# Four row additions as accumulating DMAs, and two moves around W2 and the neighbour matrix, in a four-layer graph kernel

## The reference, cut to what matters

```
x1 = x0 + LN2(h1 + ff) * g2 + be2          # layer 0: attention over the edges gives h1, then
     h1 = LN1(h + att @ Wo + bo) * g1 + be1
     ff = relu(h1 @ W1 + b1) @ W2 + b2      # W1 512 x 1024, W2 1024 x 512
x2 = x1 + h @ wc + mean_over_edges(h @ wn) + bias     # layer 1, h = relu(LN3(x1))
x3 = x2 + two best of four experts, each two rounds of mean-over-edges   # layer 2
x4 = x3 + relu(degree-weighted sum of (h @ W + b))    # layer 3
```

## Time and profile before

| | us |
|---|---|
| median of 3 runs (lowest to highest) | 477.36 (476.39 to 477.62) |
| the profiled execution, its own time | 475.42 |
| its span, first to last instruction | 473.3 |
| PE busy | 450.0 (95% of the span) |
| DVE, ACT, POOL busy | 315.1, 190.5, 165.7 |

### The profile page before, as it was taken

One profiled execution on the slowest core, in us unless ns is written; L12 is line 12 of the kernel. 1 busy time (PEld: TensorE's weight loads), 2 busy tenths in 40 slices (PEclk: granted clock), 3 DMA queues, 4 the chain that ended last, 5 costly groups with the idle time before them and its releaser, 6 DMA issues.

```text
span 473.3 us, 5934 instructions
## 1 busy us (share of the span) xinstructions
PE 450.0 (95%) x2096; PEld 327.8 (69%) x2096; DVE 315.1 (67%) x570; ACT 190.5 (40%) x265; POOL 165.7 (35%) x110
## 2 busy tenths in 40 slices
PE   7999999979899998799999999999999999999996
PEld 3456544434359886678778788888888888888765
DVE  5999868999997986958865935342262237133864
ACT  5898734555133421252632353044303342227230
POOL 4000221212233996266242444144444444344100
PEclk9999999999999999799999999999999999999999
DMA  8760000000031244004011222222220332020002
GB/s 276 190 258 1 1 2 0 24 0 0 1 111 46 89 152 156 6 16 182 3 26 64 90 89 90 89 89 112 89 90 13 117 149 77 24 89 1 0 1 89
DMA packets 22474, 34.34 MB, mean 73 GB/s; under 512 B 5680, under 2 KB 5936, under 8 KB 22448
## 3 DMA queue, kind: packets, MB, share of 16 engines
q1 hardware_dynamic: 22160, 33.85, 20.3%
q10 hardware_dynamic: 288, 0.13, 0.1%
HBM read 32.93 MB, written 1.05 MB: 72 GB/s over the span
## 4 chain that ended last, share of the span: by engine, by line
PE 70%; DVE 18%; issue 6%; ACT 2%; POOL 1%; DVEq 1%; DMA 1%; POOLq 0%
PE ps L1236 15%; PE ps L1238 15%; PE ps L1237 15%; PE ps L1298 4%; PE ps L1309 4%; PE ps L1265 3%; PE ps L1264 3%; DVE rsum L947 2%; PE ps L1386 2%; DVE stats L754 2%; PE ps L1291 2%; DVE e_sb L384 2%; DVE one_src L828 1%; PE ps L1249 1%; PE ps L1565 1%
## 5 line engine op out<-in xcount | busy, mean ns | idle before, releaser
L463 POOL TENSOR_TENSOR w_lo<-w_stage,w_hi 128x1024 fp32r<-128x1024 f32 x22 | 53.6, 2434 | 129.7 <-ACT w_hi L554 118.9
L554 ACT ACTIVATE w_hi<-w_stage 128x2048 fp32r<-128x2048 f32 x23 | 43.9, 1909 | 61.8 <-PE ps L1238 61.8
L464 POOL TENSOR_TENSOR w_lo<-w_stage,w_hi 128x1024 fp32r<-128x1024 f32 x22 | 57.3, 2604 | 0.0
L1236 PE MATMUL ps<-w_hi,hid_hi 128*128 128x512 f32 x128 | 49.9, 390 | 0.5 <-DVE hid_lo L1147 0.5
L1237 PE MATMUL ps<-w_lo,hid_hi 128*128 128x512 f32 x128 | 49.8, 389 | 0.0
L1238 PE MATMUL ps<-w_hi,hid_lo 128*128 128x512 f32 x128 | 49.8, 389 | 0.0
L1236 PE MATMUL ps<-T_hi,w_hi 128*128 128x512 f32 (+1 forms) x112 | 41.0, 366 | 0.4 <-POOL w_lo L464 0.4
L1237 PE MATMUL ps<-T_lo,w_hi 128*128 128x512 f32 (+1 forms) x112 | 40.2, 359 | 0.0
L1238 PE MATMUL ps<-T_hi,w_lo 128*128 128x512 f32 (+1 forms) x112 | 40.2, 359 | 0.0
L1145 DVE TENSOR_SCALAR tmp<-ps,bl 128x512 f32<-128x512 f32 x16 | 12.0, 749 | 39.9 <-ACT hid_hi L705 39.9
L828 DVE TENSOR_SCALAR one_src<-iota_n,edge_m,edge_w 128x256 f16 x128 | 34.1, 334 | 0.4 <-POOL edge_w L500 0.4
(11 more groups left out here) (216 smaller groups left out, 998.2 us busy)
## 6 DMA issues: line engine op xcount, KB each, us to landing
w_stage<-in_L_gnn_Wr SPq DMA_DIRECT2D x8, 1024.0 KB, 5.0
w_stage<-in_L_gnn_Wl SPq DMA_DIRECT2D x8, 1024.0 KB, 5.0
w_stage<-in_L_gnn_W SPq DMA_DIRECT2D x5, 1024.0 KB, 6.6
x_sb<-in_x SPq DMA_DIRECT2D x4, 256.0 KB, 3.7
w_q<-in_L_gnn_Wq SPq DMA_DIRECT2D x1, 1024.0 KB, 7.6
w_k<-in_L_gnn_Wk SPq DMA_DIRECT2D x1, 1024.0 KB, 10.0
w_v<-in_L_gnn_Wv SPq DMA_DIRECT2D x1, 1024.0 KB, 5.9
w_o<-in_L_gnn_Wo SPq DMA_DIRECT2D x1, 1024.0 KB, 10.3
```

The costliest lines, as they stand in the source:

```text
L463: gp.tensor_tensor(w_lo[s][:, 0:2], stage[s][:, 0:2], f32(w_hi[s][:, 0:2]), ALU.subtract)
L464: gp.tensor_tensor(w_lo[s][:, 2:4], stage[s][:, 2:4], f32(w_hi[s][:, 2:4]), ALU.subtract)\
L554: nc.scalar.activation(w_hi[u % 2][:], stage[u % 2][:], ACT.Copy).then_inc(hi_made, 1)
L1236: nc.tensor.matmul(goal, a_hi, b_hi, start=start, stop=False, **kw)
```

## The change

Four things are changed.

1. The additions of `bo`, `b2` and `be2` leave POOL's arithmetic. Each becomes one DMA of 1 MB that POOL issues: it reads the 2 KB row from HBM once for every partition and tile, and adds to what is in SBUF. `be2` is issued once LN0 has read `x_sb`, and `bo` once layer 0's transposes have read `h_sb`, both behind the split of W1A; `b2` is issued where its first tile was added. Each has one completion, which DVE waits for in every tile.
2. `bias` becomes four such DMAs of 256 KB, one for each tile, each with its own semaphore. Tile `t - 1` is issued behind the power of LN3's tile `t`, and tile 3 behind that, ahead of `split_lo(WC)`. Each waits until LN3's `normalise` has read its tile. The four rows are no longer loaded by SP, and the row of `g2` no longer waits for `bo`.
3. The degree product moves from between W2A and W2B to behind the reach product, and from PSUM bank 4 to bank 6. Its copy out moves from DVE to ACT, which also moves the copy of the reach result: both now stand behind LN3's `normalise` of tile 0. PE waits for the degree copy ahead of the transposes of tile 2.
4. WN's high and low parts get buffers of their own, where the attention's third exponential buffer was. They wait only for the attention's last use of it (`pv_done`) and no longer for W2A's products. The first expert's matrix then waits for W2A's buffer.

```diff
+    w_hi.append(place("wn_hi", [P, 4, D], F32R, rVZ + 2 * MAT))
+    w_lo.append(place("wn_lo", [P, 4, D], F32R, rVZ + 3 * MAT))
...
+        def w_free(u, first):
+            if u < 2:
+                return first
+            if u == WN:
+                return pv_done, 2 * STEPS
+            return w_spent[u - 4] if u == WN + 2 else w_spent[u - 2]
+        def home(u):
+            return 2 if u == WN else u % 2
...
+            def add_bias1(t):
+                gp.wait_ge(ln_out, ln_out_no(LN3, t))
+                gp.dma_start(x_sb[:, t, :], d["L1_gnn_bias"].unsqueeze(0).to_broadcast([P, D]), accum_op=ALU.add)\
+                  .then_inc(bias1_added[t], 16)
...
+            def add_row(name, target, done):
+                gp.dma_start(target[:], d[name].unsqueeze(0).unsqueeze(0).to_broadcast([P, NT, D]),
+                             accum_op=ALU.add).then_inc(done, 16)
...
             split_lo_tile(W1A, DT - 1)
+            gp.wait_ge(ln_out, ln_out_no(LN0, NT - 1))
+            add_row("L0_gnn_be2", x_sb, be2_added)
+            gp.wait_ge(tr_done, tr_no(T0, NT - 1))
+            add_row("L0_gnn_bo", h_sb, bo_added)
...
-            add_row(B2, 0, h_sb, b2_added)
+            add_row("L0_gnn_b2", h_sb, b2_added)
             split_lo(W2A)
-            for t in range(1, NT):
-                add_row(B2, t, h_sb, b2_added)
             split_lo(W2B)
-            for t in range(NT):
-                add_row(BETA2, t, x_sb, be2_added)
             split_lo(WN)
             for k, t in ln_order[2 * NT:4 * NT]:
                 power(ln_no(k, t))
+                if k == LN3 and t >= 1:
+                    add_bias1(t - 1)
+            add_bias1(NT - 1)
             split_lo(WC)
-            for t in range(NT):
-                gp.wait_ge(ln_out, ln_out_no(LN3, t))
-                add_row(BIAS1, t, x_sb, bias1_added)
...
             split_hi(WN)
-            act.wait_ge(reach_done, 1)
-            nc.scalar.activation(reach_2[:], ps[:, 7, 0:2 * NT]...)
             for t in range(NT):
                 normalise(LN3, t, h_sb, x_sb, ACT.Relu)
+                if t == 0:
+                    act.wait_ge(reach_done, 1)
+                    nc.scalar.activation(reach_2[:], ps[:, 7, 0:2 * NT]...)
+                    act.wait_ge(deg_done, 1)
+                    nc.scalar.activation(inv_in_row[:], ps[:, 6, :], ACT.Copy).then_inc(deg_made, 1)
...
-            v.wait_ge(deg_done, 1)
-            nc.vector.tensor_copy(inv_in_row[:], ps[:, 4, :]).then_inc(deg_made, 1)
...
-                    pe.wait_ge(diag_made, NT)
-                    pe.wait_ge(ones_made, 1)
-                    for t in range(NT):
-                        last = nc.tensor.matmul(ps[:, 4, col(t)], ones[:], tmp[:, t, 0:P], start=True, stop=True)
-                    last.then_inc(deg_done, 1)
...
             reached(NT - 1, c_hi, NT - 1, ...).then_inc(reach_done, 1)
-            pe.wait_ge(deg_made, 1)
+            pe.wait_ge(diag_made, NT)
+            pe.wait_ge(ones_made, 1)
+            for t in range(NT):
+                last = nc.tensor.matmul(ps[:, 6, col(t)], ones[:], tmp[:, t, 0:P], start=True, stop=True)
+            last.then_inc(deg_done, 1)
             w = weights(WN)
             for t in range(NT):
+                if t == NT - 2:
+                    pe.wait_ge(deg_made, 1)
```

More of the change, by code:

```diff
@@ L215, in build @@
     W_LAST = len(units) - 1
[L218 to L221, removed]
+    rows_in = [("L0_gnn_bv", 0), ("L0_gnn_g1", 2), ("L0_gnn_be1", 3), ("L0_gnn_g2", 1), ("L3_gnn_b", 0)]
+    BV, GAMMA1, BETA1, GAMMA2, B3 = range(len(rows_in))
     LN0, LN1, LN2, LN3, LN4, LN5 = range(6)
@@ L307, in build @@
         att_made = sem("att_made")
-        bo_added, b2_added, be2_added, bias1_added = sem("bo_added"), sem("b2_added"), sem("be2_added"), sem("bias1_added")
+        bo_added, b2_added, be2_added, bias1_added = sem("bo_added"), sem("b2_added"), sem("be2_added"), [sem(f"bias1_added{t}") for t in range(NT)]
         wo_done = sem("wo_done")
@@ L391, in _ @@
             sp.dma_start(w_q[:], matrix(d["L0_gnn_Wq"])).then_inc(raw_in["q"], 16)
-            row_free = {B2: (v_made, NT), GAMMA2: (bo_added, NT), BETA2: (h_ready, NT), BIAS1: (h_ready, NT),
-                        B3: (b2_added, NT)}
+            row_free = {B3: (v_made, NT)}
             def load_row(i):
@@ L424, in _ @@
             sp.dma_start(w_v[:], matrix(d["L0_gnn_Wv"])).then_inc(raw_in["v"], 16)
-            for i in (BV, BO, GAMMA1, BETA1):
+            for i in (BV, GAMMA1, BETA1):
                 load_row(i)
             sp.dma_start(w_o[:], matrix(d["L0_gnn_Wo"])).then_inc(raw_in["o"], 16)
-            ahead = {W1B: [B2, GAMMA2], W2A: [BETA2, BIAS1], FIRST_EXPERT + 1: [B3]}
+            ahead = {W1B: [GAMMA2], FIRST_EXPERT + 1: [B3]}
             for u, src in enumerate(units):
@@ L460, in split_lo @@
                 gp.wait_ge(hi_made, u + 1)
[L461 to L464, removed]
+                gp.wait_ge(*w_free(u, (wo_done, NT)))
+                s, h = u % 2, home(u)
+                gp.tensor_tensor(w_lo[h][:, 0:2], stage[s][:, 0:2], f32(w_hi[h][:, 0:2]), ALU.subtract)
+                gp.tensor_tensor(w_lo[h][:, 2:4], stage[s][:, 2:4], f32(w_hi[h][:, 2:4]), ALU.subtract)\
                   .then_inc(lo_made, 1)
@@ L552, in split_hi @@
                 act.wait_ge(stage_in[u % 2], 16 * (u // 2 + 1))
-                act.wait_ge(*(w_spent[u - 2] if u >= 2 else ((q_done, DT), (k_done, DT))[u]))
-                nc.scalar.activation(w_hi[u % 2][:], stage[u % 2][:], ACT.Copy).then_inc(hi_made, 1)
+                act.wait_ge(*w_free(u, ((q_done, DT), (k_done, DT))[u % 2]))
+                nc.scalar.activation(w_hi[home(u)][:], stage[u % 2][:], ACT.Copy).then_inc(hi_made, 1)
             def normalise(k, t, dst, src, func):
@@ L670, in _ @@
             split_hi(WN)
-            act.wait_ge(reach_done, 1)
-            nc.scalar.activation(reach_2[:], ps[:, 7, 0:2 * NT].rearrange("p (t w) -> p t w", t=NT), ACT.Copy)\
-              .then_inc(reach_out, 1)
             for t in range(NT):
                 normalise(LN3, t, h_sb, x_sb, ACT.Relu)
+                if t == 0:
+                    act.wait_ge(reach_done, 1)
+                    nc.scalar.activation(reach_2[:], ps[:, 7, 0:2 * NT].rearrange("p (t w) -> p t w", t=NT), ACT.Copy)\
+                      .then_inc(reach_out, 1)
+                    act.wait_ge(deg_done, 1)
+                    nc.scalar.activation(inv_in_row[:], ps[:, 6, :], ACT.Copy).then_inc(deg_made, 1)
                 transposed_hi(T3, 4, t)
@@ L961, in h1_start @@
                 v.wait_ge(wo_done, t + 1)
-                v.wait_ge(bo_added, t + 1)
+                v.wait_ge(bo_added, 16)
                 link(nc.vector.tensor_tensor(h_sb[:, t, :], ps[:, wo_bank(t), :], h_sb[:, t, :], ALU.add))
@@ L1031, in _ @@
                 v.wait_ge(w2_done, t + 1)
-                v.wait_ge(b2_added, t + 1)
+                v.wait_ge(b2_added, 16)
                 ins = nc.vector.tensor_tensor(h_sb[:, t, :], ps[:, t, :], h_sb[:, t, :], ALU.add)
@@ L1064, in _ @@
                 v.wait_ge(alpha_done, t + 1)
-                v.wait_ge(bias1_added, t + 1)
+                v.wait_ge(bias1_added[t], 16)
                 nc.vector.tensor_tensor(x_sb[:, t, :], ps[:, 4 + t, :], x_sb[:, t, :], ALU.add)\
@@ L1241, in weights @@
                 pe.wait_ge(lo_made, u + 1)
-                return w_hi[u % 2], w_lo[u % 2]
+                return w_hi[home(u)], w_lo[home(u)]
             def col(t):
```

9 lines of the change are left out of this document (1 added, 8 removed).

## The result

The kernel after takes **471.69 us** (median of 4 runs, 471.54 to 472.32), the kernel before on the same chip 477.44 us (4 runs, 476.39 to 477.62): a ratio of 0.989, 95% interval 0.9873 to 0.9907. That is 5.75 us faster, where 3.05 us were forecast. The profiled execution of after took 472.32 us, with a span of 470.3 us. Those two figures are the forecast's, yet we shall see that the span is so by accident.

What follows compares the result with a forecast made beforehand. PE's chain bounds the kernel, the start of W2B setting the stretch after it. Starting W2B 3.05 us earlier, with nothing added, gives 477.36 - 3.05 = 474.3 us; own range 473.5 to 475.0, full range 472.9 to 477.1.

Steps and rivals of the forecast that it cites:

- the sum: Whole kernel: 3.05 us off, nothing on; span 473.3 to 470.3, profiled execution 475.42 to 472.4, median 477.36 to 474.3 us.
- The degree product's move: Between W2A and W2B: W2B starts 3.05 us earlier; the product's 0.91 us is covered by PE's idle time at LN3.
- Rival 1: PE's clock holds at 2.4 GHz in LN3's stretch, WN's tile 0 is faster: 473.8 us or a little less; chance 0.20.
- WN's buffers: WN's split on POOL, if left in place, would delay LN2's first power, costing up to 2 us; no gain by itself.
- The landings: The 1 MB additions of bo, be2 and b2 land within 20.6 us at most, all hidden.
- An issue on POOL: One bias DMA issue on POOL ahead of WC's split takes 1.0 us, causing no stall.
- The slack at WC: Ahead of POOL's split of WC, one issue may take up to 1.3 us before PE waits.
- Rivals 2 to 4: POOL's issue at 1.3 to 2.6, near 3.2, or from 3.9 us: 475.3, 477.3, 480.9 us (at 4.94); chances 0.15, 0.11, 0.06.
- rival 3: Nothing gained: issue near 3.2 us at WC, or accumulating DMA adds work around the span; 477.3 us, chance 0.11.
- the 1.75 us priced by that rule: Bias issues meeting DVE operations of 0.75 us at most would take 1.75 us; tile 2's issue still ends at 206.4.

Runs made afterwards that it cites:

- reach_late: Kernel before with only ACT's copy of the reach result moved behind LN3's normalise of tile 0; 476.31 us, ratio 0.9998.
- before_fill: Kernel before with 11 filler products on PE between the transposes of LN3's tiles 0 and 2; 475.61 us, ratio 0.9988.
- no_deg: Kernel after with the degree product, its wait, DVE's copy and ACT's reach copy back in their old places; 475.57 us, ratio 0.9988.
- WN shared: Kernel after with WN's parts back in the shared buffers; 471.91 us, ratio 0.9903.
- WC early on ACT: Kernel after with only ACT's copy of WC moved behind tile 1's transposes, POOL's order kept; 471.82 us, ratio 0.9904.
- the degree filler: Kernel before with 8 filler products on PE ahead of the degree product, in the wait for the diagonals; 476.01 us, ratio 0.9997.
- both fillers: Kernel before with filler products both at LN3's transposes and in the wait for the diagonals; 475.30 us, ratio 0.9984.
- WC early: Kernel after with ACT's copy of WC behind tile 1's transposes and POOL's split of WC ahead of bias's last two issues; 474.40 us, ratio 0.9968.
- diag_early: Kernel before with the four diagonals ahead of DVE's small operations, the degree product left in place; 473.62 us, ratio 0.9938.
- before_again: Kernel before, unedited, run again as a yardstick; 476.02 us, ratio 0.9996.

## Why the prediction was wrong, and where it was right

**The step that failed** is the last sentence of the sum: "against the median, 477.36 - 3.05 = 474.3 us". It takes a difference worked out in one execution of 475.42 us and subtracts it from a median 1.9 us above it, as if what made those runs longer would stay. The sum, "3.05 us off, nothing on", has no term for the clock behind the wait that the change removes. The runs show such a term: 1.6 us in the one long execution profiled, and no span above 470.3 us in the 20 executions with the move and no added cost.

What the spans show is a floor and falls of the clock on top. The floor of before is 472.6 to 472.8 us (both experiments with fillers at LN3). There are three places where an execution may lose clock:

- in the attention: 0.6 us (after, 178.36 against 177.78, its clock 0.96 against 1.00), and 0.4 to 0.7 us in other profiled executions
- at LN3, when the fall is as long as in the profiled execution of before (0.77 over 190 to 205): 0.6 us, being 473.3 - 472.7
- at the degree product, behind the 2.0 us of waiting: 1.6 us

These add up where I can check them. The long execution of reach_late had all three, since its clock was 0.97 and 0.94 in the attention and 0.77 at LN3 too: 472.7 + 0.6 + 0.6 + 1.6 = 475.5 us, and its span is 475.5. The profiled executions of the group at 473.3 have one fall that counts: that at LN3, or that in the attention beside a short one at LN3 (0.89 over 190 to 205). The short one costs nothing: before_fill's profiled execution had the attention's fall alone and the same 473.4 us. The one at 474.0 (no_deg, mean clock 0.988) has both small ones. The rest is read off sums. Spans of 474.3 to 474.7 us with a mean clock of 0.993 lose less clock than that one and are no shorter; the large fall alone would fit them (472.7 + 1.6 = 474.3), and before_fill's three of 474.0 to 474.4. With one small one it gives 474.9, where spans from 474.7 to 475.5 us with 0.988 lie. None of these was profiled.

After the change the floor is 469.6 to 469.7 us, 2.9 to 3.2 us lower, where 3.05 were summed. The large fall has lost its place, as PE runs from W2A into W2B. The fall at LN3 costs nothing: the execution of the degree move alone had WN's tile 0 at the low clock and a span of 469.7, since PE catches up before normalise of tile 3, behind WC's copy, sets the pace. PE's timeline of that execution:

```profile
194.90 0.79 PE L1237 MATMUL ps<-w_hi,T_hi 128*128 128x512 f32 x1
195.49 0.63 PE L1238 MATMUL ps<-w_lo,T_hi 128*128 128x512 f32 x1
...
203.15 0.63 PE L1250 MATMUL ps<-ident,h_sb 128*128 128x128 f32 x4 [0.51 <-ACT h_sb L559]
```

Even with the products at 0.63 us PE comes to tile 3 in time to wait 0.51 us, as it did in after (0.53). Only the attention's 0.6 us is left, and 469.7 + 0.6 = 470.3 is the profiled span. That it met the forecast's 470.3 is luck: before's profiled execution had lost 0.6 us at LN3, which the change takes away, and after's lost as much in the attention, which the change doesn't touch. All 20 executions of the four kernels with the move and no added cost (after, the move alone, WN shared, WC early on ACT) span 469.2 to 470.3 us.

On the first chip three of the four runs of before, 477.36 to 477.62, are by their time long executions (475.5 of span and 2.1 around it); their spans and clocks are not on record. From 475.5 to 469.7 is 5.8 us, and 5.75 were measured. If they had all three falls, as the profiled long one had, this is 3.05 of the order of work, 1.6 and 0.6 of clock that the change gives back, and 0.6 of the attention's fall, which three of after's four runs merely happened not to have. On the other chips, where long executions were 6 of 22 at most, the move is worth 4.0 to 4.4 us by the medians. So the size of the result depends on how often before loses clock in the third place on the chip at hand. What the change takes by the order of work alone is about 3.05 us on each.

**Point by point.** The degree product's move: right, with both of its terms (2.1 and 0.9) measured apart. Rival 1, the clock at LN3, had a chance of 0.20 and a price of 0.5 us. The clock did hold in the profiled execution, but it was no separate case: in after that fall costs nothing either way, and its 0.6 us belongs to every comparison with an execution of before that had it. The clock behind the degree wait the prediction did not consider; its one trace shows 1.00 there. WN's buffers: "up to 2 us" if left; measured nothing, since DVE has tile 1's sum and statistics to do first. The landings: 11.4 to 15.8 us, inside the bound of 20.6. An issue on POOL: 0.86 to 0.90 us against 1.0. The slack at WC: 1.3 - 0.88 = 0.4 us by the prediction's terms, 0.14 as read, because the split took 5.07 us (204.50 to 209.57) and not 4.75. Rivals 2 to 4 fell with the issue's price, and rival 3's work around the span did not come. The Trainium skill ("DMA: Bandwidth & Descriptors", Specifications) gives some 1 us to the first byte from GpSimd. No row here shows the first byte; the issue's own row is 0.9 us. By "SBUF — State Buffer" (the box on DVE blocking DMA) GpSimd can't write its descriptors while a DVE operation of certain kinds holds the shared port. The two issues beside DVE's 128 x 512 operations took 0.90 and 0.89 us and the two beside a DVE all but idle 0.86, so the 1.75 us priced by that rule did not come. No run tells whether those operations hold the port.

**Not settled.** Why executions take the long form, and so unevenly (three of four on one chip, 6 of 22 and 3 of 29 on others); whether the degree filler keeps them away (12 runs without one are too few to tell from chance); one span of 474.1 with both fillers, and one of before at 476.4, which no sum of the three gives; the clocks of the first chip's runs of before.

## What to carry to other kernels

A median and a profiled execution that differ by 2 us are different executions. Before carrying a difference from one to the other, ask what the longer ones lose and where: a wait of 2 us on PE can cost its own length, and in some executions the clock of the work behind it, and both go when the wait goes; the wait of 2.2 us that WC early brought in cost both. Compare spans of like kind rather than medians when a change is worth less than the spread between executions. On GpSimd, mind what stands right behind a tiny operation whose result DVE needs: a long split there held a 0.16 us operation for 2.3 us.

## What the runs showed of the hardware that was not expected

- An accumulating DMA issued by POOL takes it 0.86 to 0.90 us by its row for 256 KB in rows of 2 KB (landing 4.0 us after), and 1.33 us for b2's 1 MB (landing 11.4 to 15.8 us for the three). POOL's next work started 0.56 and 0.88 us behind the issue's start. Two plain ones of 256 KB took 1.45 us together, and held the next work for 1.13.
- WN's load is issued while b2's addition is under way, and took 7.9 us to land; before it took 5.1.
- DVE's `ff_lo` of one tile took 5.43 us beside POOL's split of W2A, as against 0.69 for the tiles after it. It was hidden. In the same way the four diagonals of diag_early took 7.24 us beside the split of W2B and be2's additions, against 0.86 in after.
- PE's granted clock was 1.00 in one execution and 0.50 in another behind the same wait of 2.0 us, with the same work before it. A fall in the attention doesn't decide it: before_again had one (0.96 and 0.95) and 1.00 behind the wait.
